# The Hadamard product of a decoder's last FFN as two float32r products of a split operand, the subtraction on VectorE, and the lists of all engines in another order

## What is computed

```
def act_quant(x, bits=8):
    qb = float(2 ** (bits - 1))
    scale = qb / jnp.clip(jnp.max(jnp.abs(x), axis=-1, keepdims=True), EPS)
    return jnp.clip(jnp.round(x * scale), -qb, qb - 1) / scale
def h_bitlinear(x, w):
    return jnp.einsum('bsh,oh->bso', act_quant(fwht(x)), weight_quant(w))
gate = bitlinear(x, w_gate)
up = bitlinear(x, w_up)
intermediate = jax.nn.silu(gate) * up
return h_bitlinear(intermediate, w_down)
```

## Time and profile before

| | us |
|---|---|
| three runs, median (lowest to highest) | 695.84 (695.28 to 696.39) |
| the profiled execution's own time | 695.4 |
| its span, first to last instruction | 693.3 |
| PE busy in the span | 668.4 (96%) |
| DVE busy | 605.5 (87%) |
| POOL busy | 570.5 (82%) |
| ACT busy | 423.5 (61%) |

### The profile page before, as it was taken

How to read it: one execution, slowest core, us unless ns; L and a number is a source line. 1 busy time by engine, 2 the same in 40 slices (tenths; PEclk the granted TensorE clock), 3 DMA queues, 4 the chain that set the end, 5 groups by cost and what they waited for, 6 DMA issues and landing times. The chain is left out here.

```text
span 693.3 us, 13904 instructions
## 1 busy us (share of the span) xinstructions
PE 668.4 (96%) x4318; PEld 482.1 (70%) x4318; DVE 605.5 (87%) x1329; ACT 423.5 (61%) x692; POOL 570.5 (82%) x750
## 2 busy tenths in 40 slices
PE   8999999999999899998899999999999999999994
PEld 7888888754444577786688888855444477777883
DVE  5988889679999998878899999889999998888774
ACT  1765666721370686976798888830101468888985
POOL 3986988987878699994467889999988989989952
PEclk9999999999999999999999999999999999999998
DMA  8820000000400050000211111122000000000001
GB/s 309 334 107 1 2 2 2 2 1 0 182 0 0 1 213 21 2 2 1 95 62 61 61 62 62 62 75 66 0 0 1 0 1 2 16 17 17 16 17 45
DMA packets 12726, 33.39 MB, mean 48 GB/s; under 512 B 2672, under 2 KB 8048, under 8 KB 11376
## 3 DMA queue, kind: packets, MB, share of 16 engines
q1 hardware_dynamic: 12080, 31.99, 12.5%
q10 hardware_dynamic: 576, 0.53, 0.3%
HBM read 30.35 MB, written 2.16 MB: 47 GB/s over the span
## 5 line engine op out<-in xcount | busy, mean ns | idle before, releaser
L1084 PE MATMUL bank<-XT,win_late 128*128 128x256 f32 x320 | 79.8, 385 | 2.0 <-DVE ss_xc L1269 1.6
L632 DVE TENSOR_REDUCE MIX<-m_pr 128x128 f32<-128x1024 f32 x64 | 76.6, 1206 | 0.4
L1269 DVE SCALAR_TENSOR_TENSOR ss_xc<-bank,cw_late,ss_xc 128x254 f32<-128x254 f32 x144 | 67.7, 477 | 6.2 <-ACT ss_xc L1173 2.7
L577 POOL TENSOR_TENSOR m_kv<-CTXT 128x512 f32<-128x512 f32 x64 | 65.1, 1042 | 7.4 <-PE bank L609 7.2
L577 POOL TENSOR_TENSOR m_kv<-XT,CTXT 128x512 f32<-128x512 f32 x64 | 68.0, 1089 | 1.4 <-PE bank L609 1.4
L607 PE MATMUL bank<-m_kv,toep 128*128 128x512 f32 x128 | 66.3, 600 | 1.2 <-POOL m_kv L577 1.0
L609 PE MATMUL bank<-m_kv,toep 128*128 128x512 f32 x128 | 65.4, 592 | 0.0
L608 PE MATMUL bank<-m_kv,toep 128*128 128x512 f32 x128 | 65.4, 592 | 0.0
L1084 PEld LDWEIGHTS bank<-XT,win_late 128*128 128x128 f32 x320 | 56.7, 190 | 11.9 <-DVE ss_xc L1269 4.3
L1562 PE MATMUL bank<-had_last,f_ht 128*128 128x256 f32 x256 | 59.4, 379 | 0.0
L445 POOL TENSOR_TENSOR at_p<-at_p,at_mx 128x512 f32<-128x512 f32 x44 | 45.0, 1041 | 10.6 <-DVE at_mx L355 10.5
(11 more groups left out here) (255 smaller groups left out, 1946.6 us busy)
## 6 DMA issues: line engine op xcount, KB each, us to landing
MIX<-cum_rows SPq DMA_DIRECT2D x15, 512.0 KB, 3.6
toep<-toep_dram SPq DMA_DIRECT2D x2, 2048.0 KB, 12.3
X<-x_dram SPq DMA_DIRECT2D x1, 2048.0 KB, 13.8
CTXT<-ctxT_dram SPq DMA_DIRECT2D x1, 2048.0 KB, 17.5
out_dram<-f_o SPq DMA_DIRECT2D x16, 128.0 KB, 1.7
XT<-xT_dram SPq DMA_DIRECT2D x1, 1280.0 KB, 9.3
win_late<-win_dram SPq DMA_DIRECT2D x1, 1280.0 KB, 5.2
wgu<-wgu_dram SPq DMA_DIRECT2D x1, 1024.0 KB, 5.2
```

What stands on the lines that cost most here:

```text
L577: m = nc.gpsimd.tensor_tensor(KV[n % 3][:, c, :, :].rearrange("p (b j) i -> p b j i", b=HB), ki, vj, ALU.mult)
L632: nc.vector.tensor_reduce(head(MIX)[:, :, a, bass.ts(h, HB), :], PR[n % 2][:, :, :, :].rearrange("p c (b j) i -> p c b j i", b=HB), op=ALU ...
L1084: m = nc.tensor.matmul(bX[(NU * g + n) % 3][:, 0:GS_], win[:, h, off:off + P], XT[:, h, bass.ts(g, GS_)], start=(h == 0), stop=(h == C - 1))
L1269: m = nc.vector.scalar_tensor_tensor(acc[:, :, sh:S], bank[:, :, 0:S - sh], cw[:, r, n:n + 1], acc[:, :, sh:S], ALU.mult, ALU.add)
```

## The change

Four things are edited.

1. `had` is copied once by ACT into a float32r tile `had_round`, which the products use. Its elements are 1 and -1.
2. HT becomes float32r, so that `keep_h` writes H rounded. A new DVE function `rest_h(n, k)` subtracts HT from the bank and writes the rest to a new float32r tile HL. It waits for `keep_h` and for the last product that read HL.
3. `transform(n, k)` multiplies both HT and HL, eight products of 128x256 in float32r for four in float32, and waits for `h0_rest` or `h1_rest`. The waits that guarded the banks of H (`up` of half 0, `h_turn`) are on the subtraction too, instead of the copy.
4. The five engines' lists are in another order over the whole kernel. Every list has the same calls as before, but for the 32 calls of `rest_h` in `vector_order`.

```diff
@@ -525,6 +525,7 @@
                 made = nc.scalar.activation(T["w128"][:, k:k + 1], T["wscale"][:, m:m + 1], ACT.Identity, scale=scale)
             made.then_inc(s["made"], 1)
             act.wait_ge(s["staged_in"], 80)
+            nc.scalar.copy(T["had_round"][:, :, :], T["had"][:, :, :])
             nc.scalar.activation(T["bo"][:, :], T["grp"][:, :], ACT.Identity, scale=T["bias"][:, :]).then_inc(s["made"], 1)
 
         if not skip:
@@ -994,6 +995,7 @@
 
     for n, shape in (("bo", [P, P]), ("had", [P, 2, 2 * P]), ("grp", [P, P]), ("bias", [P, 1]), ("w128", [P, 3])):
         T[n] = ch.sb(n + "_last", shape)
+    T["had_round"] = ch.sb("had_round", [P, 2, 2 * P], F32R)
 
 
 GB = 2
@@ -1427,14 +1429,14 @@
 
     def two(name, shape, dt=F32, n=2):
         return [ch.sb(f"f1_{name}{k}", shape, dt) for k in range(n)]
-    bo, had = T["bo"], T["had"]
+    bo, had = T["bo"], T["had_round"]
     rnd, unrnd = ch.sb("f1_rnd", [P, 1]), ch.sb("f1_unrnd", [P, 1])
     E, Y = two("e", [P, D]), two("y", [P, D])
     U1, U2, Z = two("usum", [P, D]), two("ures", [P, D]), two("z", [P, D])
     Q, QT = two("q", [P, D], BF16), two("qt", [P, C, S], BF16)
     SL, H, H2 = two("silu", [P, FF]), two("h", [P, FF]), two("hmix", [P, FF])
     H1, V, R, W = (ch.sb("f1_" + n, [P, FF], BF16 if n == "w8" else F32) for n in ("hs1", "v", "r", "w8"))
-    HT, WT = ch.sb("f1_ht", [P, FC, S]), ch.sb("f1_wt", [P, FC, S], BF16)
+    HT, HL, WT = (ch.sb("f1_" + n, [P, FC, S], t) for n, t in (("ht", F32R), ("hl", F32R), ("wt", BF16)))
     Y2, O = two("ydown", [P, D]), two("o", [P, D])
     ST, MV, VE, RS, NR = two("st", [P, 6]), two("mv", [P, 2]), two("ve", [P, 1]), two("rs", [P, 1]), two("nr", [P, 1])
     ST3, MV3, VE3, RS3, NR3 = two("sto", [P, 6]), two("mvo", [P, 2]), two("veo", [P, 1]), two("rso", [P, 1]), two("nro", [P, 1])
@@ -1532,14 +1534,14 @@
             if n == 0:
                 pe.wait_ge(mixed["multed"], 2 * (last_of[2 if k else 0] + 1))
             if k == 0:
-                upto(pe, s["h0_kept"], n - 1)
+                upto(pe, s["h0_rest"], n - 1)
             product(n, bU[k], FF + 512 * k, f"u{k}_made")
 
         def h_turn(n, k):
             if not 0 <= n < B:
                 return
             pe.wait_ge(s["s2_made"], n + 1)
-            upto(pe, s[f"h{k}_kept"], n)
+            upto(pe, s[f"h{k}_rest"], n)
             if k == 0:
                 pe.wait_ge(s["h0_made"], min(n + 2, B))
             else:
@@ -1553,13 +1555,15 @@
         def transform(n, k):
             if not 0 <= n < B:
                 return
-            pe.wait_ge(s[f"h{k}_kept"], n + 1)
+            pe.wait_ge(s[f"h{k}_rest"], n + 1)
             upto(pe, s[f"v{k}_kept"], n)
             if k == 0:
                 pe.wait_ge(s["silu0_made"], min(n + 3, B))
             for r in range(2):
                 for i in range(2):
-                    m = nc.tensor.matmul(bV[k][:, bass.ts(r, 2 * P)], HT[:, 4 * k + 2 * r + i, :], had[:, i, :], start=(i == 0), stop=(i == 1))
+                    for part in (HT, HL):
+                        m = nc.tensor.matmul(bV[k][:, bass.ts(r, 2 * P)], part[:, 4 * k + 2 * r + i, :], had[:, i, :],
+                                             start=(i == 0 and part is HT), stop=(i == 1 and part is HL))
             m.then_inc(s[f"v{k}_made"], 1)
 
         def w_turn(n):
@@ -1747,6 +1751,15 @@
         def second(n):
             second_on(dve, nc.vector, n)
 
+        def rest_h(n, k):
+            if not 0 <= n < B:
+                return
+            dve.wait_ge(s[f"h{k}_kept"], n + 1)
+            upto(dve, s[f"v{k}_made"], n)
+            quarter = slice(4 * k, 4 * k + 4)
+            nc.vector.tensor_tensor(HL[:, quarter, :], bH[k][:, :].rearrange("p (r s) -> p r s", r=4), HT[:, quarter, :].bitcast(F32),
+                                    ALU.subtract).then_inc(s[f"h{k}_rest"], 1)
+
         def v_peak(n):
             if not 0 <= n < B:
                 return
@@ -1799,7 +1812,7 @@
             nc.vector.bn_aggr(MV3[n % 2][:, :], ST3[n % 2][:, :]).then_inc(s["stats3"], 1)
 
         return calls(skip_times=skip_times, skip_add=skip_add, add_mix=add_mix, stats=stats, aggregate=aggregate, peak=peak, step_size=step_size,
-                     scale=scale, keep_q=keep_q, multiply=multiply, first=first, second=second, v_peak=v_peak, v_step=v_step, v_scale=v_scale,
+                     scale=scale, keep_q=keep_q, multiply=multiply, first=first, second=second, rest_h=rest_h, v_peak=v_peak, v_step=v_step, v_scale=v_scale,
                      drop=drop, add_down=add_down, stats3=stats3, aggregate3=aggregate3)
 
     def gpsimd(pool):
@@ -1848,336 +1861,340 @@
...
-    a.busy(); a.qk(0, 0); a.qk(0, 1); a.value(0); a.qk(1, 0); a.qk(1, 1); a.score(0); a.qk(2, 0); a.qk(2, 1); a.score(1); a.qk(3, 0); a.qk(3, 1)
-    a.bias(); a.value(1); a.turn_p(0, 0); a.turn_p(0, 1); a.turn_p(0, 2); a.score(2); a.turn_p(0, 3); a.qk(4, 0); a.qk(4, 1); a.times_v(0, 0)
-    a.times_v(0, 1); a.times_v(0, 2); a.times_v(0, 3); a.turn_p(1, 0); a.turn_p(1, 1); a.score(3); a.turn_p(1, 3); a.qk(5, 0); a.turn_p(1, 2)
...
+    a.busy(); a.qk(0, 0); a.qk(0, 1); a.value(0); a.qk(1, 0); a.qk(1, 1); a.score(0); a.value(1); a.bias(); a.qk(2, 0); a.qk(2, 1); a.score(1)
+    a.qk(3, 0); a.qk(3, 1); a.turn_p(0, 1); a.turn_p(0, 2); a.turn_p(0, 0); a.turn_p(0, 3); a.score(2); a.qk(4, 0); a.qk(4, 1); a.times_v(0, 0)
+    a.times_v(0, 1); a.times_v(0, 2); a.times_v(0, 3); a.turn_p(1, 0); a.turn_p(1, 1); a.score(3); a.turn_p(1, 3); a.turn_p(1, 2); a.qk(5, 0)
...
-    g.first(15); g.v_peak(13); g.v_step(13); g.v_scale(13); g.second(15); g.drop(13); g.add_down(11); g.aggregate3(10); g.stats3(11); g.aggregate3(11)
-    g.v_peak(14); g.add_down(12); g.v_step(14); g.v_scale(14); g.stats3(12); g.drop(14); g.aggregate3(12); g.v_peak(15); g.v_step(15); g.v_scale(15)
-    g.add_down(13); g.drop(15); g.stats3(13); g.add_down(14); g.aggregate3(13); g.stats3(14); g.aggregate3(14); g.add_down(15); g.stats3(15)
-    g.aggregate3(15)
...
+    n.times_q(30); g.multiply(1, 1); g.rest_h(0, 0); g.scale(3); g.add_mix(5); n.add_up(29); g.stats(5); n.times_q(31); g.peak(4); g.keep_q(3)
+    g.aggregate(5); n.add_up(30); g.rest_h(0, 1); g.multiply(2, 0); g.step_size(4); g.skip_times(6); g.multiply(2, 1); g.skip_add(6); g.scale(4)
+    g.v_peak(0); g.add_mix(6); g.peak(5); g.rest_h(1, 0); g.stats(6); g.step_size(5); g.v_step(0); g.scale(5); g.aggregate(6); g.skip_times(7)
...
+    g.stats3(10); g.multiply(15, 1); g.aggregate3(10); g.v_peak(13); g.add_down(11); g.first(15); g.rest_h(14, 0); g.v_step(13); g.v_scale(13)
+    g.rest_h(14, 1); g.second(15); g.drop(13); g.stats3(11); g.add_down(12); g.aggregate3(11); g.v_peak(14); g.rest_h(15, 0); g.v_step(14)
+    g.v_scale(14); g.rest_h(15, 1); g.stats3(12); g.aggregate3(12); g.add_down(13); g.drop(14); g.stats3(13); g.v_peak(15); g.aggregate3(13)
+    g.v_step(15); g.v_scale(15); g.add_down(14); g.drop(15); g.stats3(14); g.aggregate3(14); g.add_down(15); g.stats3(15); g.aggregate3(15)
 
...
@@ -2192,7 +2209,7 @@
       "eps_added rstd normed x_turned x_kept").split()
 F1 = ("consts mix_turned skip_made skip_free summed stats1 stats2 eps_added rstd offset normed peaks inv_made scaled shifted "
       "q_made q_turned q_kept g0_made g1_made u0_made u1_made silu0_made silu1_made gs_made "
-      "h0_made h1_made s1_half s1_made s2_half s2_made h0_turned h1_turned h0_kept h1_kept v0_made v1_made v0_kept v1_kept "
+      "h0_made h1_made s1_half s1_made s2_half s2_made h0_turned h1_turned h0_kept h1_kept h0_rest h1_rest v0_made v1_made v0_kept v1_kept "
       "v_peaks hi_made sh_made fs_made rounded w_made w_turned w_kept downed down_free "
       "stats31 stats3 eps_added3 rstd3 offset3 o_made skip_in").split()
 M1 = "kv_made conved multed reduced staged_in made".split()
```

More of the change, by code:

```diff
@@ L1928, in tensor_order @@
-    g.mix_turn(5); g.skip(5); g.gate(2, 0); g.gate(2, 1); g.up(2, 1); g.h_turn(0, 0); n.mix(31); g.transform(0, 0); g.q_turn(3); g.up(2, 0)
-    g.h_turn(0, 1); g.mix_turn(6); g.gate(3, 1); g.skip(6); g.transform(0, 1); g.h_turn(1, 0); g.up(3, 1); g.gate(3, 0); g.q_turn(4); g.h_turn(1, 1)
-    g.mix_turn(7); g.skip(7); g.transform(1, 0); g.up(3, 0); g.transform(1, 1); g.w_turn(0); g.q_turn(5); g.gate(4, 0); g.gate(4, 1); g.up(4, 1)
-    g.h_turn(2, 0); g.down(0); g.h_turn(2, 1); g.up(4, 0); g.transform(2, 0); g.transform(2, 1); g.mix_turn(8); g.skip(8); g.h_turn(3, 0)
@@ L1932, in tensor_order @@
-    g.gate(5, 0); g.gate(5, 1); g.h_turn(3, 1); g.up(5, 0); g.w_turn(1); g.up(5, 1); g.transform(3, 1); g.down(1); g.transform(3, 0); g.h_turn(4, 1)
-    g.q_turn(6); g.w_turn(2); g.h_turn(4, 0); g.q_turn(7); g.gate(6, 0); g.up(6, 1); g.mix_turn(9); g.skip(9); g.up(6, 0); g.gate(6, 1)
-    g.transform(4, 0); g.transform(4, 1); g.down(2); g.h_turn(5, 0); g.gate(7, 0); g.up(7, 1); g.w_turn(3); g.q_turn(8); g.gate(7, 1); g.up(7, 0)
```

(18 more changed lines are left out.)

594 lines of the change are left out of this document (296 added, 298 removed).

## The result

Six runs each on one chip: 698.5 us (697.72 to 700.49) with the change against 695.82 (694.7 to 696.39) before, a ratio of 1.0044 with a 95% interval of 1.0029 to 1.0060. The profiled execution took 699.24 us, its span is 697.3. The forecast was 699.9, slower. The total lies in its range, but two of its terms were wrong by more than 2 us each, with opposite signs, so that part of the match is luck. How that was found is the subject of what follows.

A forecast was written before the change was run, and what follows sets the result against it. PE bounds the last FFN before the change, DVE after it. Stretch +4.85, tail -0.8, lists 0 make +4.05 on the profiled 695.4 us, 699.45; with 0.44 for the median, 699.9 us, range 692.5 to 704.0.

The forecast's parts named there:

- The bound and the direction: Last FFN: DVE replaces PE as the limit and the kernel gets slower; chance of slower 0.62.
- PE's saving: Last FFN's Hadamard products: 0.70 to 0.79 us saved per half, 29 halves, 20 to 23 us off PE.
- The price of the rest: Each new DVE subtraction in the last FFN costs 0.60 us start to start, though 0.68 long.
- The stretch: From 560 us to block 15's last butterfly: 18.5 us added to DVE, 16.65 idle, 3.0 staying idle; ends 4.85 later.
- the 3.0: DVE's idle time that stays unused from 560 us on, taken as 3.0 us out of 1.2 to 4.8.
- first rival: Last FFN: DVE sheds avoidable length in additions and drops, 4.9 us, and POOL sets the end; 691.5 us, chance 0.20.
- The tail: From block 15's last butterfly to the last peak of V: 7.8 us before, 0.8 less after.
- The lists elsewhere: New order in the stages ahead of the last FFN: taken as 0, with 2 us either way for the range.
- The forecast's own sign of being wrong: Stage ends ahead of 480 us lying over 2 us from where they were would show the forecast wrong.
- The sum: Whole kernel: 4.85 for the stretch less 0.8 for the tail, other edits and lists 0, so +4.05 us.
- DVE keeps up: Another name for the first rival: in the last FFN POOL sets the end, 691.5 us, chance 0.20.
- order elsewhere: Rival: new order in earlier stages removes half of PE's 8.4 us idle, -4.2, so 695.7 us; chance 0.15.

The follow-up runs named there:

- e5: e1 without the subtractions, both float32r products reading the rounded H, so the rest of H is left out of the computation: 691.85 us, ratio 0.9950 to before.
- e7: e1 with each subtraction from block 1 on done on half the columns, so half of the rest is left out: 692.1 us, ratio 0.9955 to before.
- e10: e1 with every subtraction done twice, the first time into a tile nobody reads: 715.03 us, ratio 1.0285 to before.
- e1: The changed kernel with the lists of before up to a cut in mid second mixer, the changed order behind it: 696.48 us, ratio 1.0015 to before.
- e11: e1 with three list edits at the two places where PE stood longest (two in DVE's list, one in PE's): 695.14 us, ratio 0.9997 to before.
- e12: e11 with two more places of DVE's list reordered: 696.86 us, ratio 1.0010 to before.
- e6: e1 with the 16 additions of the skip moved from DVE to PE, as a product with the identity: 701.68 us, ratio 1.0081 to before.
- e9: e1 with the copy of the turned, quantised rows and its clamp moved from DVE to ACT: 698.02 us, ratio 1.0030 to before.
- e2: The kernel before, functions unedited, with the changed order up to the cut in mid second mixer: 697.73 us, ratio 1.0035 to before.
- e8: The kernel before, functions unedited, with the changed order only up to the middle of the first mixer's first products: 697.35 us, ratio 1.0034 to before.

## Why the forecast was right, and where it wasn't

**The bound and the direction: right.** PE ceased to be the limit and DVE became it (windows and waits above, e5, e7, e10). DVE's share from 560 us is 95.5%, a little under the 96% or more of the forecast; PE is at 87% (98 us; the forecast said 88 to 91), its longest waits are for the subtraction and the drop, and the last butterfly came at 675.6 for "about 677".

**PE's saving: 20 to 23 us forecast, 14.7 measured** between POOL's first butterfly and block 15's last (122.12 to 107.46 us busy). The spacing was right (0.118). Counted from each start to the next, or to the record's own end where the next comes later, the products fell from 51.3 to 33.1 us, from 1.75 to 1.11 per half where 0.94 to 1.03 were forecast: at the end of a group the last record's own 0.28 us now often has nothing beside it. The other groups grew by 3.5 us; that these are the same gaps and the low clock is likely, but not taken apart. It cost nothing, as PE had room.

**The price of the rest: right.** 0.60 us from start to start in the rows, 0.59 in e10's time. At its whole length each would have cost 0.68, and e10 30 x 0.08 = 2.4 us more. The Trainium skill ("VectorE: DVE Perf Modes", The DRAIN you can't avoid) has the next operation wait until the pipe is empty, but adds that one that is not held back starts earlier, which the prediction left out. The trace shows the second case: 290 of DVE's 315 instructions in the stretch start before the last one has ended, by 0.08 us on average.

**The stretch: +4.85 us forecast, +0.5 measured in the changed kernel, +0.7 in e1.** This is the step that failed: the sum 30 x 0.60 + 0.5 - 16.65 + 3.0 takes DVE's other instructions to cost what they cost before. Both traces between the same two instructions, before first:

```profile
548.70:672.10 123.40, 122.12 (x762) 94.15 (x761) 106.53 (x285) 101.00 (x165) 109.74 (x137) 1.00 0.04 12
```

```profile
551.70:675.60 123.90, 107.46 (x762) 79.19 (x762) 118.88 (x316) 100.66 (x164) 109.75 (x139) 0.98 0.04 12
```

DVE got 18.5 us of work by the forecast, but its busy time rose by 12.35; 11.85 of it went into idle time, where 13.65 were forecast (16.65 less 3.0 left idle; 5.0 were left). So the idle time took 1.8 us less than forecast, but the load was 6 us smaller. One of the two stretches from which the forecast took the 3.0 doesn't bear on it: from 360 to 420 us PE was the fullest engine (59.51 of 60.00), not DVE (57.53). The load by its records, cut at the ends of the windows: lengths 124.5 and 142.6 us, +18.1 (subtractions +20.43, additions of the skip -2.52, the down addition more with its statistics +0.6, all else -0.4). Of the 2.52, 0.7 is one addition fewer between the two points (12 took 8.44 us, 11 took 5.92), and 1.8 is shorter ones. The overlap of neighbours rose from 18.0 to 23.7 us, by 5.7, which leaves +12.35. Of that 30 x 0.08 = 2.4 is in the 0.60; the other 3.3 come from other instructions that once stood after an idle spot and now follow one another closely: 61 of 283 did not overlap before, 24 of 314 after. So here the nearly full engine worked through the same list faster than its records with idle time between them suggest. The forecast's first rival had named the shrinking additions (762 ns each, 551 now) and drops (797, 777 now), 4.9 us in all; they gave 2.4, about half, and the overlap, which no rival had, gave more.

**The tail: -0.8 forecast, +0.5 measured.** From the last butterfly to the last peak: 7.78 us before, 8.28 after. In e1, with the same order there and the clock at 1.00, it is 6.65, in e11, e12 and e7 6.62 to 6.66: -1.1, a little more than forecast. The 1.6 us between go with the low clock from 675 to 678; e6 and e9, whose clock fell at this place as well, have 8.2 and 8.3.

**The lists elsewhere: 0 forecast, +2.4 measured** (e2, e8), outside the 2 us allowed. The forecast's own sign of being wrong came true here: stage ends ahead of 480 us lie over 2 us later (the first mixer begins 2.0 us late, the state-space layer's last input product 3.2, at 450.26 for 447.02). The forecast looked for PE's idle time that a new order might win, and found nothing for either sign. It did not look the other way: for long instructions that had been moved in front of something that PE waits for. `sign0` is in the diff, its 1.9 us in the trace.

**The sum.** Forecast: 4.85 - 0.8 + 0 = +4.05 in the trace. Measured: 1.1 for what lies behind the cut (e1), 2.4 for the lists ahead of it (e2), 3.5 together; the trace of one execution shows 4.0, the ratio of the whole change makes 3.1 [2.0, 4.2]. A term too high by 3 and one too low by 2.4 hid each other: that the total fell near the forecast is luck. Of the rivals, "DVE keeps up" had half of the reason why the load shrank, but the FFN came out between it and the forecast; "order elsewhere" was the right place with the wrong sign.

## What to carry to other kernels

When work goes from a full engine to one with idle time, count the idle time, and also what closes up: overlap of neighbours and contention both shrink the receiving engine's list as it fills. When a change brings new orders, go through the diff for long instructions that have moved, and see what stands behind them in the queue: order was more than half of this loss. When runs of one kernel scatter, set their times beside their mean granted clocks. And split such a change at a point where both orders agree before believing a total that came out right.
